# Convolution stage: which products run in parts, where their low parts are made, and smaller moves around them

## The reference

```python
kv  = v[:, :, :, None, :] * x2[:, :, None, :, :]            # 8 x 8 products of channels per head
y   = irfft(rfft(kv, n=1024) * rfft(k, n=1024))[..., :512]  # causal convolution along L = 512
y   = y + kv * skip
out = einsum('bhijl,bhil->bhjl', y, x1)                     # sum over i
```

## Time and profile before

| | |
|---|---|
| median of three runs | 3137.66 us |
| profiled execution, its span | 3134.95 us, 3132.9 us |
| convolution stage (until PE's first feed-forward matmul, L587) | 0 to about 590 us |
| busy share in 50.9 to 590 us: PE, DVE, POOL, ACT | 99.9%, 83%, 85%, 52% |
| TensorE clock granted in the stage (tenths on the page) | 9 or more of 10 |

### The profile page before, as it was taken

How to read it: one execution, slowest core, us unless ns; L and a number is a source line. 1 busy time by engine, 2 the same in 40 slices (tenths; PEclk the granted TensorE clock), 3 DMA queues, 4 the chain that set the end, 5 groups by cost and what they waited for, 6 DMA issues and landing times.

```text
span 3132.9 us, 49607 instructions
## 1 busy us (share of the span) xinstructions
PE 3091.6 (99%) x18229; PEld 2653.6 (85%) x18229; DVE 2148.0 (69%) x5489; ACT 1324.7 (42%) x3249; POOL 1140.3 (36%) x1176
## 2 busy tenths in 40 slices
PE   8999999999999899999999999999999999999999
PEld 5777677789899689999999999999998888888887
DVE  7888888655455688888888888888888433333342
ACT  4554554433344455555555555555555311111111
POOL 8988888354344422222222222222201011000010
PEclk9999999999999999999999999999999999999999
DMA  4444442288777621111111111111101200000000
GB/s 149 138 135 134 125 125 81 81 301 299 209 229 228 233 72 48 48 48 48 48 42 48 48 48 48 42 41 48 35 28 61 84 28 27 28 27 28 27 14 14
DMA packets 124974, 277.67 MB, mean 89 GB/s; under 512 B 18312, under 2 KB 18960, under 8 KB 124736
## 3 DMA queue, kind: packets, MB, share of 16 engines
q1 hardware_dynamic: 95712, 178.54, 17.5%
q0 software_dynamic: 29024, 95.97, 9.3%
HBM read 170.04 MB, written 104.42 MB: 88 GB/s over the span
## 4 chain that ended last, share of the span: by engine, by line
PE 95%; DVE 3%; POOL 1%; ACT 1%; DMA 1%; issue 0%; SPq 0%; POOLq 0%; DVEq 0%
PE f_Y L513 5%; PE g_PH L2470 4%; PE g_PH L2472 4%; PE g_PH L2471 4%; PE g_O L2486 4%; PE g_O L2485 4%; PE g_O L2484 4%; PE t_U L1748 4%; PE t_U L1749 4%; PE t_U L1750 4%; PE t_T L1724 3%; PE f_Y L519 3%; PE f_Y L521 3%; PE f_Y L518 3%; PE t_PO L1734 2%; PE t_S L1713 2%
## 5 line engine op out<-in xcount | busy, mean ns | idle before, releaser
L1874 ACT ACTIVATE t_pr<-t_sm,t_nb 128x256 f32<-128x256 f32 x512 | 256.6, 502 | 409.3 <-DVE t_nb L2081 409.3
L2255 POOL TENSOR_TENSOR t_r<-t_r 128x256 f32<-128x256 f32 x128 | 94.5, 738 | 732.1 <-DVE t_r L2060 414.1
L2542 DVE CAST g_hh<-g_hf 128x512 fp32r<-128x512 f32 x128 | 54.6, 427 | 430.8 <-PE g_O L2486 427.3
L1303 POOL TENSOR_TENSOR c_kf<-c_vt,c_ct 128x512 f32<-128x512 f32 x256 | 282.6, 1121 | 53.0 <-PE f_Y L513 53.0
L2513 ACT ACTIVATE g_hf<-g_PH,b1g 128x512 f32<-128x512 f32 x128 | 88.2, 689 | 493.7 <-PE g_PH L2472 493.7
L2091 DVE TENSOR_SCALAR t_pr<-t_pr,t_rw 128x256 f32<-128x256 f32 x512 | 238.8, 466 | 18.1
L518 PE MATMUL f_Y<-c_kh,c_th 128*128 128x512 f32 x448 | 224.1, 500 | 2.8 <-ACT c_kh L742 1.7
L1028 DVE TENSOR_TENSOR c_z<-f_Y,c_ct 128x512 f32<-128x512 f32 x256 | 174.4, 681 | 53.6 <-PE f_Y L513 53.6
L1748 PE MATMUL t_U<-t_voh,t_oth 128*128 128x512 f32 x512 | 202.3, 395 | 0.0
L2470 PE MATMUL g_PH<-g_xh,g_w 128*128 128x512 f32 x512 | 202.0, 395 | 0.0
L1749 PE MATMUL t_U<-t_voh,t_otl 128*128 128x512 f32 x512 | 201.6, 394 | 0.0
(11 more groups left out here) (346 smaller groups left out, 9849.1 us busy)
## 6 DMA issues: line engine op xcount, KB each, us to landing
xs<-c_zero SPq DMA_DIRECT2D x71, 256.0 KB, 4.6
f_xg<-xs SPq DMA_DIRECT2D x71, 256.0 KB
ys<-f_yt POOLq DMA_DIRECT2D x71, 256.0 KB, 3.4
f_xg<-xn SPq DMA_DIRECT2D x40, 256.0 KB
c_xt<-x SPq DMA_DIRECT2D x32, 256.0 KB, 3.5
c_cr<-ctx SPq DMA_DIRECT2D x32, 256.0 KB, 3.9
c_ct<-ctxh SPq DMA_DIRECT2D x32, 256.0 KB, 4.8
c_t<-kt SPq DMA_DIRECT2D x32, 256.0 KB, 4.9
```

What stands on the lines that cost most here:

```text
L1303: gp.tensor_tensor(o, iv, ic, ALU.mult).then_inc(*GP("kv", n))
```

## The change

- All four blocks of a unit are split: `split` on ACT runs for mb 0 to 3, and `conv` has three fp32r matmuls for every product; the plain float32 product is gone. `kh` and `kl` grow to four blocks for each of two units. `kf` shrinks from eight blocks to four, without a unit index, so `product` n waits for `low` n-4 and no longer for PE.
- `low` runs for all four blocks: on DVE for (u, mb) = (0,0), (0,2), (1,0), (1,3), on POOL for the other four.
- The filters' low parts are no longer subtracted on POOL from head 4 on. Once, the 32 filters are loaded flat, rounded on ACT, subtracted on DVE (`filters_lo`), written to DRAM, and in eight DRAM-to-DRAM transfers (one a head, heads 0 to 6, after `store_filters`) spread so that a shifted read gives the Toeplitz block. SP loads it (`tlf`) and ACT copies it to `tl`, once a head.
- One `pow` on 128x2 serves both norms (`powers`); the work on the finished rows (`shift_rows`, `norm_rows`, `turn_rows`, `logit`, `store_xn`, `best`) moves to later steps; `weigh` moves from step (0,0) to (0,2) on DVE, `residual` to the next head's (0,1) on POOL; the choice of experts on DVE is spread over several steps.

```diff
@@ low_by, filter_by (new)
+def filter_by(K, h):
+    return K.VE if h == 0 else K.GP if h < 4 else K.AC
+def low_by(K, u, mb):
+    return K.VE if (u, mb) in ((0, 0), (1, 0), (0, 2), (1, 3)) else K.GP
@@ sync_front
+        if h > 3:
+            w.wait_ge(*AC["tl", h - 2 if h > 5 else -1])
+            w.wait_ge(*Q["kw"]["tlt", h // 4])
+            sp.dma_start(m.tlf[:, h % 2, :], tlr[h]).then_inc(*Q[f"u{h % 2}"]("tlf", h))
+    def spread_filters(c):
+        w.wait_ge(*Q["kw"]["tlt", c - 1] if c > 1 else Q["kw"]["klo"])
+        r = slice(4 * c, 4 * c + 4)
+        sp.dma_start(tlw[r], d["klo"][r, :].unsqueeze(1).to_broadcast([4, 128, 640])).then_inc(*Q["kw"]("tlt", c))
+                if u == 1 and lb == 0 and h == 0:
+                    store_filters()
+                if u == 1 and lb == 1 and h < 7:
+                    spread_filters(h + 1)
-                if u == 1 and lb == 3 and h:
+                if u == 0 and lb == 3 and h > 1:
+                    store_xn(h - 2)
+                if u == 1 and lb == 3 and h == LAST:
                     store_xn(h - 1)
@@ tensor_front
-            if mb > 1:
-                w.wait_ge(*GP["kv", n])
-                t = pe.matmul(Y, m.t[:, h % 3, c], m.kf[:, v, mb, :], start=False, stop=mb == lb)
-                continue
-            w.wait_ge(*(GP if h else VE)["tl", h])
+            w.wait_ge(*filter_by(K, h)["tl", h])
-            w.wait_ge(*(GP if mb else VE)["kl", n])
+            w.wait_ge(*low_by(K, u, mb)["kl", n])
-                if u == 0 and lb == 0 and h > 1:
+                if u == 0 and lb == 2 and h > 1:
                     turn_rows(h - 2)
-                if u == 0 and lb == 2 and h > 1:
+                if u == 1 and lb == 0 and h > 1:
                     logit(h - 2)
@@ scalar_front
+    def filter_lo(h):
+        w.wait_ge(*Q[f"u{h % 2}"]["tlf", h])
+        w.wait_ge(*PE["y", 8 * (h - 2) + 7])
+        copy(m.tl[:, h % 2, :], m.tlf[:, h % 2, :]).then_inc(*AC("tl", h))
     def split(h, u, mb):
-        if mb > 1:
-            return
+                if u == 0 and lb == 0 and h > 1:
+                    shift_rows(h - 2)
+                    norm_rows(h - 2)
+                if u == 0 and lb == 3 and 3 <= h < LAST:
+                    filter_lo(h + 1)
-                if h and u == 1 and lb == 3:
+                if h == LAST and u == 1 and lb == 3:
                     shift_rows(h - 1)
                     norm_rows(h - 1)
@@ vector_front
+    def filters_lo():
+        ve.memset(m.klo[:, 0:128], 0.0).then_inc(*VE("klo0"))
+        w.wait_ge(*AC["khi"])
+        ve.tensor_tensor(m.klo[:, 128:640], m.kq[:, :], f32(m.khi[:, :]), ALU.subtract).then_inc(*VE("klo"))
+    low(0, 0, 2)
+    filters_lo()
-                if u == 0 and lb == 0 and more:
+                if u == 0 and lb == 2 and more:
                     weigh(h + 1)
-                gather_i(h, u, lb, UNITS[n] if n < len(UNITS) and lb == 0 else None)
+                gather_i(h, u, lb, UNITS[n] if n < len(UNITS) and lb in ((0, 2) if u else (0, 3)) else None)
@@ gpsimd_front
+    def powers(h):
+        w.wait_ge(*AC["var", h + 2])
+        w.wait_ge(*AC["var0", h - 1])
+        gp.tensor_tensor(m.rsb[:, h % 2, :], m.rsb[:, h % 2, :], mhalf, ALU.pow).then_inc(*GP("rs", h + 2))
     def product(h, u, mb):
-        if mb == 0:
-            w.wait_ge(*VE["kl", n - 8])
-        w.wait_ge(*PE["y", 4 * (2 * h + u - 2) + 3])
+        w.wait_ge(*low_by(K, 1 - u, mb)["kl", n - 4])
     for n in range(4):
         product(*UNITS[n])
-        if n == 1:
+        if n % 2:
             low(*UNITS[n])
-                if u == 0 and lb == 1:
+                if u == 0 and lb in (1, 2):
                     low(*UNITS[n])
-                if u == 1 and lb == 0 and more:
+                if u == 1 and lb == 3 and n < len(UNITS):
+                    low(*UNITS[n])
+                if u == 1 and lb == 0 and h < 3:
                     filter_lo(h + 1)
-                if u == 1 and lb == 2 and more:
-                    residual(h + 1)
+                if u == 0 and lb == 1 and h:
+                    residual(h)
```

More of the change, by code:

```diff
@@ L768, in shift @@
         w.wait_ge(*GP["rs", h])
[L769 removed]
+        ac.activation(m.nm[:, s, :], m.ag[:, s, 0:1], ACT.Copy, scale=root(m, h)).then_inc(*AC("nm", h))
     def mean_rows(i):
@@ L783, in spread_rows @@
         w.wait_ge(*AC["ba0", i])
-        ac.activation(m.rs0[:, s, :], m.ag0[:, s, 1:2], ACT.Copy, scale=1.0 / D, bias=EPS).then_inc(*AC("var0", i))
+        ac.activation(root_rows(m, i), m.ag0[:, s, 1:2], ACT.Copy, scale=1.0 / D, bias=EPS).then_inc(*AC("var0", i))
     def shift_rows(i):
         s = i % 2
-        w.wait_ge(*GP["rs0", i])
-        ac.activation(m.nm0[:, s, :], m.ag0[:, s, 0:1], ACT.Copy, scale=m.rs0[:, s, :]).then_inc(*AC("nm0", i))
+        w.wait_ge(*(GP["rs", i + 3] if i + 3 < NHC else GP["rs0", i]))
+        ac.activation(m.nm0[:, s, :], m.ag0[:, s, 0:1], ACT.Copy, scale=root_rows(m, i)).then_inc(*AC("nm0", i))
     def norm(h):
@@ L809, in split @@
         w.wait_ge(*PE["y", 4 * (2 * h + u - 2) + 3])
-        copy(m.kh[:, u, mb, :], m.kf[:, u, mb, :]).then_inc(*AC("kh", n))
+        copy(m.kh[:, u, mb, :], m.kf[:, mb, :]).then_inc(*AC("kh", n))
     def shared_hi(i):
@@ L864, in scalar_front @@
                     norm(h + 1)
-                if u == 0 and lb == 0 and h > 1:
-                    turned_rows(h - 2)
                 if u == 0 and lb == 3 and more:
@@ L1123, in vector_front @@
                     skips(h + 1)
-                if u == 0 and lb == 3 and h > 1:
+                if u == 1 and lb == 0 and h > 1:
                     best(h - 2)
@@ L1129, in vector_front @@
                     gates(h // 8 - 1)
+                if u == 1 and lb == 3 and h > 8 and h % 8 == 2:
+                    hot(h // 8 - 1, 0)
+                if u == 1 and lb == 3 and h > 8 and h % 8 == 3:
+                    hot(h // 8 - 1, 1)
+                    counts(h // 8 - 1)
+                if u == 1 and lb == 3 and h > 8 and h % 8 == 4:
+                    gates2(h // 8 - 1)
                 if h == LAST and u == 1 and lb == 0:
@@ L1214, in vector_front @@
             choose(3)
+            hot(3, 0)
+            hot(3, 1)
+            counts(3)
         if n == 6:
             gates(3)
+            gates2(3)
         if n == 8:
@@ L1352, in gpsimd_front @@
                 n = (2 * h + u) * 4 + lb + 4
-                if u == 1 and lb == 3 and h + 2 < NHC:
-                    power(h + 2)
+                if u == 1 and lb == 3 and h < LAST:
+                    if h == 0:
+                        power(2)
+                    elif h + 2 < NHC:
+                        powers(h)
+                    else:
+                        power_rows(h - 1)
                 if u == 1 and lb == 1:
@@ L1357, in gpsimd_front @@
                         low(*UNITS[n])
-                if u == 1 and lb == 2 and h:
+                if u == 1 and lb == 2 and h == LAST:
                     power_rows(h - 1)
@@ L2613, in layouts @@
     return a
-DMA_COUNTS = ("sk", *(f"x{i}" for i in range(4)), *(f"c{i}" for i in range(3)), "r0", "r1", "t0", "t1", "t2", *(f"o{i}" for i in range(4)), "z",
+DMA_COUNTS = ("sk", "kw", "u0", "u1", *(f"x{i}" for i in range(4)), *(f"c{i}" for i in range(3)), "r0", "r1", "t0", "t1", "t2", *(f"o{i}" for i in range(4)), "z",
               "cc", "n0", "n1", "w0", "w1", "ti", *(f"g{i}" for i in range(RING)), "q0", "q1", "a0", "a1", *(f"s{i}" for i in range(RING)),
```

84 lines of the change are left out of this document (55 added, 29 removed).

## The result

The changed kernel takes 3180.15 us (median of 4 runs, 3178.89 to 3181.89); the kernel before, run beside it, 3137.89 (4 runs, 3137.17 to 3139.12). The ratio is 1.0135, with a 95% interval of 1.0122 to 1.0147: 42 us slower, where 13 us faster was forecast, and outside the range of 3109 to 3143. The profiled execution took 3178.89 us, its span is 3177.1 against 3132.9 us.

What follows compares the result with a forecast made beforehand. PE was taken to bound the convolution, with POOL late first: 6.6 us lost by head 9, 20.5 and 0.5 regained, net 14.4 less, 1.9 given back, so a median of 3125 us; range 3109 to 3143.

Steps and rivals of the forecast that it cites:

- PE: what goes: Convolution on PE: 192 plain products become three-part ones, 29.8 us less in all; head falls from 17.96 to 17.03 us.
- the first rival: PE sets the pace nearly throughout, meetings cost POOL 0.9 us a head or less: about 3112 us; chance 0.17.
- POOL: what comes: POOL's bare work a head: two more lows, no filter from head 4, one power; 14.19 becomes 14.91 us.
- The meetings: DVE instructions with two SBUF inputs delay POOL: five a head at 0.40 us, 2.0 us a head.
- The third rival: Slower: POOL pays DVE's whole length, 0.70 us a meeting, 3.5 a head: 3167 us; chance 0.20.
- Buffers: `product`'s 53.0 us wait for PE goes; POOL may run up to three steps ahead of DVE, hiding the extra lows.
- ACT: Roundings and filter copy make 12.2 of 17.03 us a head; 2.1 us of slack in the row chain; 0 taken.
- The choice in pieces: Choice of experts on DVE: takes away a burst that PE never waited for; nothing.
- The start: Prologue: one more low and a wait for its rounding; the loop starts at 22.3 us and not 20.2.
- SP and DMA: One more load a head and eight filter spreads, heads 0 to 6: zero, bound 1 us each, 8 us.
- The sum: Following POOL: 6.6 us lost by head 9, then 20.5 and 0.5 gained; net 14.4 less, 1.9 given back.
- second rival: Gain eaten early, trickles late: meetings at 0.5 us each, POOL needs 17.4 from head 9; 3136 us; chance 0.15.

Runs made afterwards that it cites:

- PE alone: Changed kernel with roundings and low parts of blocks 2 and 3 left out, PE's work complete, plus 28 small filter spreads: 3111.84 us (3133.96 with large spreads).
- all orders: Changed kernel with finish before DVE's low, POOL's low behind its next product, ACT's variance and exponential moved, `weigh` first in head 0, small spreads: 3122.46 us, ratio 0.9962.
- the filters on POOL: "all orders" with the filters' low parts made on POOL in every head, without the way through DRAM: 3167.5 us, ratio 1.0111.
- both orders: Changed kernel with DVE's finish ahead of the low part of (h,1,3), POOL's low behind its next product, ACT's second statistic ahead of a rounding: 3140.31 us.
- filters' low later: "all orders" with DVE's low parts of block 2 and of the flat filters behind its first multiplication: 3127.49 us, ratio 0.9971.

## Why the prediction was wrong

- **PE: what goes.** Right. 17.03 us a head was predicted, 17.09 is what PE takes when nothing holds it. That the run with PE alone took 3111.84, next to the 3112 of the first rival, is in part luck: it still lost 6.6 us by head 1.
- **POOL: what comes.** Right in work: 14.91 predicted, 0.15 more for the power of 128x2 (0.67 start to start, not 0.52). With meetings 16.9 was predicted; POOL works 16.63 in the changed kernel and 17.1 in "all orders".
- **The meetings.** 2.0 us a head predicted, 1.95 measured in "all orders", 2.4 (five at 0.48) with the filters on POOL. The mean of 0.40 held only because one of five meetings met no product or low part of POOL. The third rival, 0.70 each, did not happen, and "slower" came true without it. The prediction said that 0.48 does not fit the rule of the Trainium skill by which the later one fully blocks (SBUF — State Buffer, "Who interferes with whom"). The rows of "all orders" fit it better than that: the DVE instructions that stretch, 0.83 to 1.34 us long for 0.68, each end 0.56 to 0.59 us after the POOL instruction that was running, as if they had waited for its end, and POOL's next one then takes 0.48 longer. So both may be blocked in turn. What neither the rule nor the prediction foresaw is the start: there DVE did not get its turn after one instruction of POOL but after seven, 8.65 us.
- **Buffers. This step failed.** That "POOL may run up to three steps ahead of DVE" is right for the one wait that went: its products now wait 3.8 us in all. That this "hides the extra lows" is wrong. It did not follow which waits took that wait's place. In step (1,1) POOL needs the rounding of the product that it has just made, and on ACT that rounding stands behind the row statistics, these behind `finish`, and that on DVE behind the low part of a POOL product. Each of these hand-overs is short (1.17, 1.32, 2.10 us), and each engine's sum is below its head. I summed engines and never went round the loop: the steady head was 18.46, and with both orders altered it is 17.09. One link was new and in the diff: lb = 3 in the list of `gather_i` for u = 0, which is just ahead of `finish`. The other was there before: `low` at (1,1) on POOL, ahead of its product. Its wait stands in the rows (19.7 us over 32 times), and the prediction took it as a place where meetings are free.
- **ACT. This step failed too.** It followed one chain, from the row statistics to PE's turn of the rows, found 2.1 us of slack and took 0. The chain was the right one to look at: it took DVE's low as 0.8 and did not ask what that low waits for. It waits 2.10 us, for ACT's rounding of a product that POOL has just made, and works 1.11. PE stands 1.15 us a head in the very wait on `xb` that the prediction named.
- **The choice in pieces, "nothing".** Wrong twice. In this kernel the three choice heads take 4.8, 6.2 and 5.5 us more than a steady head, since ACT's exponential now stands ahead of a norm that PE waits for. In a kernel whose heads are full, the pieces are worth 11 us against a burst.
- **The start.** 2.1 us predicted, 9.1 lost by head 1. Only POOL was followed. POOL itself is 2.9 us later than before when its loop starts (its product at 23.09 for 20.19), 0.8 more than predicted, and then waits 3.15 us for a low part of DVE. DVE is what is late: its longest row, 5.26 us, was taken as an exception, and it grew with the length of POOL's unbroken run.
- **Heads 2 to 9.** 18.15 was predicted for heads 3 to 8 as POOL's sum. They took 19.66 from head 4 on: the ring's 18.46 and the 1.24 us low part of a feed-forward weight on POOL, that lies in it, make 19.70 (worked out, not tested alone). With the ring open most of them are 17.9 to 18.25.
- **SP and DMA, zero.** Right for this kernel (0.4 us of waits, no measurable gain from small spreads), but for a reason that I did not give: the ring hid it. At PE's pace the seven large spreads cost 17 us inside the stage, twice the bound of 8.
- **The sum.** The forecast had PE's turn of head 9 at 192.8 and 22 heads at 17.03 behind it, so the turn of head 31 at 567.5. Measured were 206.0 and 620.6. So 13 us are missing up to head 9 and 40 behind it; against PE's 17.09, the three choice heads take 20.5 of these and the 19 others 18.1. The sign of the prediction for its second rival, a steady head over 17.5, came true as well, and not by its mechanism, as the meetings cost POOL less than 2.5 us a head.
- **A match that is partly luck.** "All orders" takes 3122.46, close to the forecast of 3125. Its pace is the forecast one, 17.09 for 17.03. But its turn of head 31 is 9.3 us earlier than before, where the forecast counts 12; the rest of the match lies in the scatter behind the stage.

## What to carry to other kernels

When a change takes the bound engine's work away, sum the other engines, and then also walk once round every closed loop of orders (who waits for whom, through which engine's queue, one head later), with the wait of each hand-over and not only the work. Look for the next loop too: here a second one was only 0.4 us shorter. Ask of every less urgent instruction that is put ahead of another on an engine that runs in order what it waits for itself. And do not judge the parts of such a change by the whole: the three parts that were undone here one by one (the filters through DRAM, the choice in pieces, one power) were each worth keeping, and five moves of order and smaller spreads turned 42 us lost into 12 us gained.

## What the runs showed of the hardware

- A DVE instruction with two SBUF inputs stood 8.65 us in the start of the changed kernel, 6.08 in that of "all orders" and 5.48 in that of "filters' low later", as long as POOL ran without pause, and POOL's instructions beside it were not stretched. In the steady heads of "all orders" such an instruction takes up to 0.66 us longer and costs POOL 0.48, though POOL runs without pause there too. The runs don't show what decides which of the two it is.
- Two tiny DVE instructions of the choice took about 1 us beside a busy POOL, the cast of 128x16 1.08 and the difference of 128x8 0.99, longer than the 0.68 of a whole block alone. Each ended less than 0.1 us after the POOL instruction that ran beside it, which looks like a wait for it; that was not tried.
- Behind a DRAM-to-DRAM transfer of 1280 KB the next issue of its queue took 9.42 us, and the load of `x` behind it 11.7 us until ACT could start on it, against a median of 3.4 to landing. Transfers of 320 KB, with the same total, held nothing back that PE could feel: its heads stay at 17.08 to 17.09.
- After waits of 4.58, 4.59 and 4.59 us PE ran at the lower clock (0.50 from 374.70 to 380.31 in head 18), and lost another 1.3, 2.7 and 2.1 us by it. After the 1.15 us of a steady head the clock shows 1.00 and nothing is lost.
- `pow` on POOL takes 0.67 us for 128x2 and 0.52 for 128x1: the second element adds 0.15.
